# Exponentials per PSUM bank, deferred V transposes and a context sum in four parts, in an attention and feed-forward kernel

## What is computed

```python
xn = _layernorm(x, axis=-1)
kqv = xn @ W_kqv.T                       # 1024 -> 3 x 1024
k_, q_, v_ = jnp.split(kqv, 3, axis=-1)  # each to (B, 16 heads, S, 64)
bias = alibi_slopes(H)[:, None, None] * rel
score = jnp.einsum('bhsd,bhnd->bhsn', q, k) / scale + bias[None]
attn = jax.nn.softmax(score, axis=-1)
s = jnp.einsum('bhsn,bhnd->bhsd', attn, v)
...
global_context = xn.mean(axis=1, keepdims=True)     # over the 4096 positions
gf = _global_net(global_context, ...)
out = xn
for _ in range(3):
    tf = _coupling_net(out, ...)          # 1024 -> 1024 -> 512 -> 256 -> 1, gelu
    combined = 0.7 * gf + 0.3 * tf
    coupling = 0.1 + adaptive_range * (combined - 0.5) * 2.0
    out = out + coupling * _twist(out)
x = x + s * _silu(out)
```

## Time and profile before

| what | before |
|---|---|
| median of 3 runs | 2889.6 us |
| lowest, highest of them | 2887.43, 3022.56 us |
| the profiled execution, device time | 2874.52 us |
| its span on the slowest core (the eight: 2859.2 to 2872.9) | 2872.9 us |
| mean granted TensorE clock on that core (the eight: 0.888 to 0.897) | 0.888 |
| PE busy | 2191.4 us, 76% |
| ACT busy | 1361.7 us, 47% |
| DVE busy | 827.3 us, 29% |
| exponentials of the attention (L480) | 497 on PA and 475 on PC, 1080.5 us |
| chain that ended last, by engine | PE 54%, DVE 15%, ACT 11%, issue 8%, DMA 5% |
| DVE waits for the last value matmul (L502 on L457) | 615.1 us |

### The profile page before, as it was taken

One profiled execution on the slowest core, in us unless ns is written; L12 is line 12 of the kernel. 1 busy time (PEld: TensorE's weight loads), 2 busy tenths in 40 slices (PEclk: granted clock), 3 DMA queues, 4 the chain that ended last, 5 costly groups with the idle time before them and its releaser, 6 DMA issues.

```text
span 2872.9 us, 29564 instructions; the slowest of 8 cores (2859.2 to 2872.9 us)
## 1 busy us (share of the span) xinstructions
PE 2191.4 (76%) x8647; PEld 884.4 (31%) x8756; DVE 827.3 (29%) x1315; ACT 1361.7 (47%) x1394; POOL 100.9 (4%) x150
## 2 busy tenths in 40 slices
PE   0245889888898888888988984688888888874665
PEld 0232223232222222222222223433333333323454
DVE  1566322111111000110000004624353443545333
ACT  0221444666767786768889890033333333324000
POOL 1000000000000000000000000000000000002332
PEclk9667889999999999999999995699999999995555
DMA  9500210000000000000000004444544444424665
GB/s 185 161 30 8 52 23 17 22 8 15 8 8 8 8 8 1 8 8 8 8 8 5 3 8 143 150 114 95 116 105 99 114 96 114 106 66 128 205 205 169
DMA packets 343951, 190.02 MB, mean 66 GB/s; under 512 B 303419, under 2 KB 321981, under 8 KB 343694
## 3 DMA queue, kind: packets, MB, share of 16 engines
q1 hardware_dynamic: 323470, 160.08, 21.0%
q0 software_dynamic: 3696, 11.27, 2.7%
q10 hardware_dynamic: 16640, 16.78, 2.0%
HBM read 165.30 MB, written 36.96 MB: 70 GB/s over the span
## 4 chain that ended last, share of the span: by engine, by line
PE 54%; DVE 15%; ACT 11%; issue 8%; DMA 5%; DVEq 4%; POOL 1%; SPq 0%; another core or an unknown queue 0%; ACTq 0%; POOLq 0%
PE PA L720 12%; ACT PBH L480 9%; PE PC L472 7%; PE PA L472 6%; PE PBp L455 5%; PE PC L388 4%; PE PBp L457 3%; PE PD L455 3%; PE PD L457 3%; DMA XT<-x 3%; PE PA L388 2%; DVE STATE L836 2%; DVE TMP L827 2%; DVE SBF L805 2%; DVEq L839 2%
## 5 line engine op out<-in xcount | busy, mean ns | idle before, releaser
L480 ACT ACTIVATE PBH<-PA,ebias_s 128x1024 bf16<-128x1024 f32 x497 | 553.3, 1113 | 340.0 <-PE PA L472 311.0
L480 ACT ACTIVATE PBH<-PC,ebias_s 128x1024 bf16<-128x1024 f32 x475 | 527.2, 1110 | 145.4 <-PE PC L472 136.9
L720 PE MATMUL PA<-SBF,W1S 128*128 128x512 bf16 x1505 | 346.9, 390 | 22.9 <-DVE SBF L805 17.0
L472 PE MATMUL PC<-QT,KT 64*128 64x512 bf16 x950 | 290.6, 386 | 86.3 <-ACT PBH L480 58.4
L472 PE MATMUL PA<-QT,KT 64*128 64x512 bf16 x994 | 305.7, 388 | 58.5 <-ACT PBH L480 31.8
L731 ACT ACTIVATE H<-PA,b1c_s 128x512 bf16<-128x512 f32 x192 | 131.9, 687 | 332.6 <-PE PA L720 332.6
L455 PE MATMUL PD<-PBH,VB 128*65 128x512 bf16 x528 | 209.6, 397 | 19.0 <-DVE SRW L502 12.3
L827 DVE TENSOR_TENSOR TMP<-PD,STATE 128x512 f32<-128x512 f32 x192 | 123.7, 686 | 348.2 <-PE PD L819 342.8
L720 PEld LDWEIGHTS PA<-SBF,W1S 128*128 128x128 bf16 x1536 | 151.9, 100 | 218.0 <-issue 50.2
L502 DVE COPY SRW<-PBp 65x1024 f32<-65x1024 f32 x32 | 39.1, 1221 | 615.1 <-PE PD L457 615.1
L457 PE MATMUL PD<-PBH,VB 128*65 128x512 bf16 x528 | 208.3, 395 | 0.0
(11 more groups left out here) (109 smaller groups left out, 1819.1 us busy)
## 6 DMA issues: line engine op xcount, KB each, us to landing
W1S<-w1b_s SPq DMA_DIRECT2D x192, 256.0 KB, 2.8
W2S<-w2b_s SPq DMA_DIRECT2D x96, 256.0 KB, 2.8
XTs<-x SPq DMA_DIRECT2D x8, 2048.0 KB, 31.9
sraw_s<-SRW SPq DMA_DIRECT2D x64, 256.0 KB
XT2s<-x SPq DMA_DIRECT2D x16, 1024.0 KB, 4.9
XT<-x SPq DMA_DIRECT2D x32, 512.0 KB, 4.1
SINB<-sraw_s ACTq DMA_DIRECT2D x16, 1024.0 KB, 5.4
out<-OUT SPq DMA_DIRECT2D x32, 512.0 KB, 2.8
```

Of the source, the lines that this page charges most:

```text
L472: inst = TE.matmul(RING[rp + sub], lhs, QT[b][hh * 64:(hh + 1) * 64, sc * SC2:(sc + 1) * SC2], start=True, stop=True)
L480: inst = SE.activation(out=PBH[slot][:], in_=PFULL[rp // 2][:], func=AF.Exp, bias=ebias[:, h * 32 + nt: h * 32 + nt + 1], scale=1.0 / 32.0)
L720: inst = TE.matmul(HALF[slot][:], W1S[wslot][:, ft * 128:(ft + 1) * 128], sbf[:, ft * TC:(ft + 1) * TC], start=(ft == 0), stop=(ft == NF - 1))
```

## The change

Three things are done.

1. The ring is used bank by bank. Each score matmul takes one bank, signals by itself, and has an exponential of its own over 512 columns into one of twelve tiles PB_; the value matmuls read two of these and wait for the second. `ring_next_pair` and the 1024-column tiles PBH go.
2. The transposes of a V unit are put on a list (`pvt`) and are issued behind the matmuls and the copy of the next unit (`flush_vt`), or at the end of the generator. A V unit takes one turn. The rate of 48 turns stays.
3. The eight reductions of XB are taken out from between the stages; two of them are issued behind each of pairs 0 to 3, and the scaling behind pair 3.

```diff
@@ -132,7 +132,6 @@
     QT = [at(f"QT{i}", [128, S], BF16, 128 + 8 * i) for i in range(2)]
     VB = [at(f"VB{i}", [128, 32 * 130], BF16, 144 + 8.25 * i) for i in range(2)]
     PB_ = [at(f"PBUF{i}", [128, 512], BF16, 160.5 + 1 * i) for i in range(12)]
-    PBH = [at(f"PBH{i}", [128, 1024], BF16, 160.5 + 2 * i) for i in range(6)]
     SRW = [at(f"SRW{i}", [128, 1024], F32, 172.5 + 4 * i) for i in range(2)]
     VSTG = [at(f"VSTG{i}", [128, 512], F32, 180.5 + 2 * i) for i in range(2)]
     vsj = [0]
@@ -313,12 +312,18 @@
                     inst = VE.tensor_copy(out=dst, in_=src)
                     vXBe.inc(inst)
                     lnslot_tok[slot] = vXBe.n
-        VE.wait_ge(vXBe.h, vXBe.n)
-        for ft in range(NF):
-            VE.reduce_sum(gct[:, ft:ft + 1], XB[:, ft * S:(ft + 1) * S], axis=mybir.AxisListType.X)
-        VE.drain()
-        inst = VE.tensor_scalar(out=gctb[:], in0=gct[:], scalar1=1.0 / S, scalar2=None, op0=AOP.mult)
-        vGctx.inc(inst)
+        def gctx_chunk(pi):
+            if pi >= 4:
+                return
+            if pi == 0:
+                VE.wait_ge(vXBe.h, vXBe.n)
+            for ft in range(2 * pi, 2 * pi + 2):
+                VE.reduce_sum(gct[:, ft:ft + 1], XB[:, ft * S:(ft + 1) * S], axis=mybir.AxisListType.X)
+            if pi == 3:
+                VE.drain()
+                inst = VE.tensor_scalar(out=gctb[:], in0=gct[:], scalar1=1.0 / S,
+                                        scalar2=None, op0=AOP.mult)
+                vGctx.inc(inst)
 
         TE.wait_ge(sW.h, W0_TOTAL)
         TE.wait_ge(sWG.h, WG_TOTAL)
@@ -339,19 +344,6 @@
                 TE.wait_ge(sem.h, val)
             return r
 
-        PFULL = [PA, PC]
-
-        def ring_next_pair():
-            r = ring_pos[0]
-            if r % 2:
-                r = (r + 1) % 4
-            for q in (r, r + 1):
-                if ring_tok[q] is not None:
-                    sem, val = ring_tok[q]
-                    TE.wait_ge(sem.h, val)
-            ring_pos[0] = (r + 2) % 4
-            return r
-
         OUTH = [[PBp[0:65, 0:512], PBp[0:65, 512:1024]],
                 [PD[0:65, 0:512], PD[0:65, 512:1024]]]
         out_tok = [(vXBe, max(lnslot_tok[2], lnslot_tok[3])), None]
@@ -369,6 +361,25 @@
                     first[0] = False
 
             n0p = N0_PAIR[p]
+            pvt = []
+
+            def flush_vt():
+                while pvt:
+                    j, cp_tok, sc = pvt.pop(0)
+                    r2 = ring_next()
+                    TE.wait_ge(vKV.h, cp_tok)
+                    for k in range(4):
+                        inst = TE.transpose(RING[r2][:, k * 128:(k + 1) * 128],
+                                            VSTG[j][:, k * 128:(k + 1) * 128], identf[:])
+                    tKQ.inc(inst)
+                    VE.wait_ge(tKQ.h, tKQ.n)
+                    for hh in range(2):
+                        inst = VE.tensor_copy(
+                            out=v4[b][:, 4 * sc:4 * sc + 4, hh, 0:64],
+                            in_=RING[r2].rearrange("p (k d) -> p k d", d=128)[:, :, hh * 64:hh * 64 + 64])
+                        vKV.inc(inst)
+                    ring_tok[r2] = (vKV, vKV.n)
+
             units = []
             for fpi, fp in enumerate([8 + p, p]):
                 tc0 = (n0p * 128) // 512 if fpi == 1 else 0
@@ -393,6 +404,9 @@
                     gate_ve()
                     VE.wait_ge(tKQ.h, tKQ.n)
                     inst = VE.tensor_copy(out=dst[:, tc * 512:(tc + 1) * 512], in_=RING[r])
+                    vKV.inc(inst)
+                    ring_tok[r] = (vKV, vKV.n)
+                    flush_vt()
                 else:
                     sc = tc
                     base = 2 * D + p * 128
@@ -409,28 +423,15 @@
                     inst = VE.tensor_copy(out=VSTG[j][:], in_=RING[r])
                     vKV.inc(inst)
                     ring_tok[r] = (vKV, vKV.n)
-                    cp_tok = vKV.n
-                    yield
-                    r2 = ring_next()
-                    TE.wait_ge(vKV.h, cp_tok)
-                    for k in range(4):
-                        inst = TE.transpose(RING[r2][:, k * 128:(k + 1) * 128],
-                                            VSTG[j][:, k * 128:(k + 1) * 128], identf[:])
-                    tKQ.inc(inst)
-                    VE.wait_ge(tKQ.h, tKQ.n)
-                    for hh in range(2):
-                        inst = VE.tensor_copy(
-                            out=v4[b][:, 4 * sc:4 * sc + 4, hh, 0:64],
-                            in_=RING[r2].rearrange("p (k d) -> p k d", d=128)[:, :, hh * 64:hh * 64 + 64])
-                    r = r2
-                vKV.inc(inst)
-                ring_tok[r] = (vKV, vKV.n)
+                    flush_vt()
+                    pvt.append((j, vKV.n, sc))
                 yield
+            flush_vt()
 
         SC2 = 512
         NSCP = 4
-        pb_av_tok = [0] * 6
-        pb_exp_tok = [0] * 6
+        pb_av_tok = [0] * 12
+        pb_exp_tok = [0] * 12
         srw_tok = [0, 0]
         sridx = [0]
 
@@ -445,20 +446,21 @@
                 def emit_attnv(flush=False):
                     while pend:
                         hh, pnt, pj = pend.pop(0)
-                        s0 = hh * 3 + (pj % 3)
-                        TE.wait_ge(sExp.h, pb_exp_tok[s0])
+                        s0 = hh * 6 + (pj % 3) * 2
+                        TE.wait_ge(sExp.h, pb_exp_tok[s0 + 1])
                         if not started[hh] and out_tok[hh]:
                             osem, oval = out_tok[hh]
                             TE.wait_ge(osem.h, oval)
                         st = not started[hh]
                         stop = flush and all(x[0] != hh for x in pend)
                         TE.matmul(OUTH[hh][0], v4[b][:, pnt, hh, 0:65],
-                                  PBH[s0][:, 0:512], start=st, stop=stop)
+                                  PB_[s0][:], start=st, stop=stop)
                         inst = TE.matmul(OUTH[hh][1], v4[b][:, pnt, hh, 0:65],
-                                         PBH[s0][:, 512:1024], start=st, stop=stop)
+                                         PB_[s0 + 1][:], start=st, stop=stop)
                         started[hh] = True
                         tAV.inc(inst)
                         pb_av_tok[s0] = tAV.n
+                        pb_av_tok[s0 + 1] = tAV.n
 
                 for nt in range(N0_PAIR[p], NT):
                     for hh in range(2):
@@ -466,25 +468,23 @@
                         if nt < N0[h]:
                             continue
                         lhs = KT[b][hh * 64:(hh + 1) * 64, nt * 128:(nt + 1) * 128]
-                        rp = ring_next_pair()
                         for sub in range(2):
                             sc = 2 * scp + sub
-                            inst = TE.matmul(RING[rp + sub], lhs,
+                            r = ring_next()
+                            inst = TE.matmul(RING[r], lhs,
                                              QT[b][hh * 64:(hh + 1) * 64, sc * SC2:(sc + 1) * SC2],
                                              start=True, stop=True)
-                        tSC.inc(inst)
-                        SE.wait_ge(tSC.h, tSC.n)
-                        slot = hh * 3 + (jj[hh] % 3)
-                        if pb_av_tok[slot]:
-                            SE.wait_ge(tAV.h, pb_av_tok[slot])
-                        inst = SE.activation(out=PBH[slot][:], in_=PFULL[rp // 2][:],
-                                             func=AF.Exp,
-                                             bias=ebias[:, h * 32 + nt: h * 32 + nt + 1],
-                                             scale=1.0 / 32.0)
-                        sExp.inc(inst)
-                        pb_exp_tok[slot] = sExp.n
-                        ring_tok[rp] = (sExp, sExp.n)
-                        ring_tok[rp + 1] = (sExp, sExp.n)
+                            tSC.inc(inst)
+                            SE.wait_ge(tSC.h, tSC.n)
+                            slot = hh * 6 + (jj[hh] % 3) * 2 + sub
+                            if pb_av_tok[slot]:
+                                SE.wait_ge(tAV.h, pb_av_tok[slot])
+                            inst = SE.activation(out=PB_[slot][:], in_=RING[r], func=AF.Exp,
+                                                 bias=ebias[:, h * 32 + nt: h * 32 + nt + 1],
+                                                 scale=1.0 / 32.0)
+                            sExp.inc(inst)
+                            pb_exp_tok[slot] = sExp.n
+                            ring_tok[r] = (sExp, sExp.n)
                     emit_attnv()
                     for hh in range(2):
                         if nt >= N0[2 * p + hh]:
@@ -540,6 +540,7 @@
                     gen_k = None
             if p < 7:
                 kqv_tok[p + 1] = vKV.n
+            gctx_chunk(p)
 
         GP.wait_ge(tAV.h, tAV.n)
         GP.wait_ge(vSR.h, vSR.n)
```

## The result

| | before | after |
|---|---|---|
| median | 2891.6 us (10 runs) | 2840.5 us (10 runs) |
| ratio, 95% interval | 1 | 0.9827 [0.9815, 0.9839] |
| ACT busy, share of the span | 1361.7 us, 47% | 1463.9 us, 52% |
| exponentials | 972 of 1024 columns | 1944 of 512 columns |

The change makes the kernel 1.7% faster, 50 us. In three of the ten executions of each kernel the cores of one die had a lower clock, and the ratio is taken from the others. The two profiled executions differ by 34 us only (2874.5 and 2840.1 us): that of the kernel before was 15 us under its median.

What follows compares the result with a forecast made beforehand. PE was taken as the fuller engine in the early pairs, ACT as nearly full in the last. Nine terms, largest -32, +23 and -21, summed to -21 us: 2889.6 to 2869 us; own range 2850 to 2885, 8 in 10 within 2812 to 2935.

Steps and rivals of the forecast that it cites:

- earlier start: Ahead of pair 0: moving the eight reductions out from between the stages ends PE's wait there, -32 us.
- stalls behind the reductions, with clock: Behind pairs 0 to 3: unit copies wait behind moved reductions on DVE, stalling PE, +23 us, plus +6 at 1.2 GHz.
- exponentials halved, steps with nothing between: 339 two-headed steps of pairs 4 to 7 with nothing put between: each 0.035 us longer, +12 us (bound +149).
- units in the ring: 57 K, Q or V units between two-headed steps, pairs 5 to 7: 0.35 to 0.4 us saved each, -21 us.
- changes of stretch: At 32 changes of stretch: one score matmul less before ACT starts, 0.21 us each, -7 us.
- V transposes: 24 sets of transposes, now behind another unit: 0.65 us each instead of 0.8, -4 us.
- early pairs: Early pairs: fewer waits for V's staging copy and some 17 bursts of units in the better ring, -6 us.
- fewer turns: Pair 5: units end sooner, leaving nine single-headed steps without units at a lower clock; with some in pair 4, +8 us.
- Rivals 1 and 2: ACT's starts don't overlap: 3006 us, chance 0.14; or starts lie 0.60 to 0.63 us apart: 2887 to 2928 us, chance 0.15.
- Rival 3: The split reductions cost 47 us instead of 29, or the units gain nothing, or both: 2887 to 2908 us, chance 0.12.
- Rival 4: The reductions are mostly hidden (-23) and 0.45 us is gained at all 126 units (-31): 2815 us, chance 0.13.

Runs made afterwards that it cites:

- e2: The changed kernel with the eight reductions back in one loop between the stages; 0.9815 of the kernel before, 53 us faster.
- e4: The kernel before with only the ring of single banks and exponentials of 512 columns; 0.9779 of the kernel before, 64 us faster.
- e6: The changed kernel with 36 turns of units instead of 48; 0.9787 of the kernel before, about 12 us faster than the changed kernel.

## Why the prediction was right in sign and wrong in size

The forecast had nine terms. Held against the ends of pairs and the kinds of steps, in the whole change:

| term | forecast | measured | from |
|---|---|---|---|
| earlier start | -32 | -33 | end of pair 0 |
| stalls behind the reductions, with clock | +29 | +35 | pairs 1 to 4, after against e2 |
| exponentials halved, steps with nothing between | +12 | -12 | table of e4, see below |
| units in the ring | -21 | -18 | table of e4 |
| changes of stretch | -7 | +2 to +5 | the last steps of the stretches in pairs 4 to 7, half of the 32: 4.13 us before, 4.23 in e4, 4.44 in the change |
| V transposes | -4 | -9 | 20 at 0.91 above a plain step, now 18 at 0.53 above a V unit |
| early pairs | -6 | -13 | pairs 1 to 3, e2 against before |
| fewer turns | +8 | 0 | window of pair 5, e6 |
| sum | -21 | about -47 | the attention: -48 |

The exponentials' term is off by 24 us. The other errors, up to some 10 us each, go both ways and nearly cancel, which was luck.

**The size of the exponentials' term.** This is the step that failed: +12 us forecast, -12 measured. It was 339 steps times the difference between a step after, 2.344 us, and a step before, 2.31, and both were off. For the step after, the prediction had both bounds and chose the lower one, 4 x 0.586, from the only pair of 512-column activations that stood back to back. In a long queue the mean is less: a plain step takes 2.30 us in pair 7 of the changed kernel, and 2.33 in pairs 4 to 7 of e4. That is about 5 us of the 24 (308 x 0.017). The greater part, about 17 us (308 x 0.056), is a mistake of method: the 2.31 us of before came from pair 7 alone and were applied to all steps, which take 2.37 on average. In pairs 4 to 6 a plain step of the kernel before takes 2.38 to 2.40 us; in the ring of single banks it takes 2.31 to 2.35 there (e4). A good half of the 17 us, some 10, lies right behind the units: in the kernel before the first plain step behind a unit or a set of transposes takes 2.58 us on average and the second 2.16, and in e4 they take 2.32 and 2.30. So a unit upset the alternation of the two pairs of banks beyond its own step. The 1.95 us that the prediction took for a unit came from a whole stretch and held this already. If these 10 us are put down to the units, they gained 28 us for 21 forecast, and the steps away from them gained 2 (2.35 us before, 2.34 in e4) where 12 were to be lost: still the largest error.

**The transposes.** They were costed by PE's 0.60 us and a late fourth score. The prediction saw at the units that the pair rule skips a bank, and left it out at the transposes, where it turns the next scores to banks that ACT is still reading. In e4 a set costs 0.3 us above a plain step where it cost 0.9. Deferred behind a unit, as in the change, it costs 0.5; that the wait for two casts comes there on top of a unit's is argued only. So the second part of the change takes back some of the first: from e4 to e2 the attention gets 7 us longer, and the totals, 0.9779 and 0.9815, point the same way with intervals that overlap a little.

**Fewer turns.** The run that the prediction meant, in the third stretch of pair 5, was not without units: the last V unit stands at its second step and the last transposes at its fifth. The seven steps behind that unit took 1.29 us each at the 2.4 GHz level, not 1.95. The prediction took the clock from the one such run it had seen. In the fourth stretch of pair 5, which has the same work, the level was 1.2 GHz from 960 to 977 us, as before. What separates the two runs isn't settled. Where the clock fell, PE had just waited 2.06 us behind the change of stretch (to 960.45); in the third stretch the eight matmuls of the V unit stand in that place, ahead of 893.3 us. No kernel tested this.

**The changes of stretch.** A stretch of pair 7 was to change by 31 x 0.035 - 0.21 = +0.9 us and changed by less than 0.3. The gap of ACT shrank from 1.42 to 1.21 us as forecast, but the time from the last step's first exponential to the next stretch grew from 3.54 to 3.86 us; the last step now has four starts and not two before the flush, which would explain it but was not tested. The term belongs with the halved exponentials, and together they are near 0 in pair 7.

**What held.** The unit: 0.35 to 0.4 forecast, 0.35 on average (4.17 to 3.82), and 0.39 in pair 6. The reductions: the place, the cause (casts behind them in DVE's order, PE out of banks), 6.74 us for 6.9 at the end of pair 1, and that the whole move is worth next to nothing. The first stretch of pair 6, 93.2 us for 94. Rivals 1 and 2, that ACT's starts cost more, fell: 0.57 to 0.59 us per start. The estimate of 613 ns, worked out from the Trainium skill ("ScalarE: Activation LUTs", What ACT_TABLE_LOAD costs), is higher than the starts of any plain step of pair 7. Rival 3 fell: the reductions cost 35 us and not 47, and the units gained. Rival 4 was right in one half (more from ring and units) and wrong in the other (reductions hidden).

**What stays open.** The early pairs gained 13 us for 6 forecast; bursts of units, one-headed steps and clock are mixed there, and no kernel took them apart. The last part of the kernel differs by up to 15 us from one profile to another at changed clocks, which no edit here explains.

## What to carry to other kernels

Before a finer split is charged with its starting cost, look at whether the engine idles at the hand-over of the coarse one: halved exponentials cost 71 us in a ring of pairs and came with a gain of 64 in a ring of single banks, where a set of transposes no longer turns the next scores to banks that ACT is still reading. Take the length of an undisturbed step from the stage where it will be used, not from the quietest one. Work for an in-order engine is put where nothing that another engine needs stands behind it; split into parts in a busy stretch, 34.7 us of it cost 35 us, and whole behind the last pair that has such work, nothing that shows.

## What the runs showed of the hardware

- Queued activations of 512 columns with a bias column start 0.57 to 0.59 us apart in the plain steps of pair 7, while each record shows 0.69 us after a gap and up to 0.93 us in a full queue. The records of the changed kernel's 1944 add up to 1538 us and cover 1143.
- Score matmuls of two heads, on rows 0 to 63 and 64 to 127, can start within 0.01 us of each other, as in e4 here (ACT then takes both of PA and after them both of PC, so the row of PC is the other head's):

```profile
1208.95 0.51 PE L459 MATMUL PA<-QT,KT 64*128 64x512 bf16 x1
1208.96 0.51 PE L459 MATMUL PC<-QT,KT 64*128 64x512 bf16 x1
1209.31 0.38 PE L459 MATMUL PA<-QT,KT 64*128 64x512 bf16 x1
```

  The Trainium skill ("TensorE: Matmul & The Clock Gate", Part 3) has matmuls on different rows of the array run at the same time; the trace agrees. Of the 1944 score matmuls of the changed kernel 141 start within 0.03 us of the one before, in the kernel before 37.
- After a PE wait of 6.74 us the next eight matmuls took 3.57 us where eight take 1.89 otherwise: the granted clock was at its 1.2 GHz level (0.50 from 332.3 to 339.1 us). In each of the four stalls of the changed kernel the clock was at that level by the end of the wait, and stayed there for 4 to 7 us more.
